# One product of an attention kernel's keys: three fp32r products of high and low parts replaced by one native fp32 product

## The reference, cut to what matters

```
q_big = einsum('bshk,hkq->bshq', q_hk, w_kc_q)
q_r   = einsum('bshq,hqr->bhsr', q_big, W_qr)
k_r   = einsum('bld,hdr->bhlr', kv_rope, W_kr)      # the keys' product
scores = einsum('bhsr,bhlr->bhsl', q_r, k_r)
attn  = softmax(scores)
ctx_c = einsum('bhsl,bld->bhsd', attn, kv_rope)
```

## Time and profile before

| | |
|---|---|
| median of 3 runs | 674.84 us (673.44 to 675.44) |
| the profiled execution's own time | 677.15 us |
| its span, first to last instruction | 675.4 us |
| mean granted TensorE clock | 0.995 |
| PE busy | 653.5 us (97%), 2870 instructions |
| DVE busy | 543.9 us (81%) |
| ACT busy | 356.8 us (53%) |
| POOL busy | 259.7 us (38%) |

### The profile page before, as it was taken

The page is one execution under the profiler, slowest core; times in us unless marked ns, Lnnn a source line. Parts: engine busy times, 40 slices in busy tenths (PEclk is TensorE's granted clock), DMA queues, the critical chain, the costliest instruction groups (busy, mean ns, idle before and its releaser), DMA issues.

```text
span 675.4 us, 9297 instructions
## 1 busy us (share of the span) xinstructions
PE 653.5 (97%) x2870; PEld 377.5 (56%) x2870; DVE 543.9 (81%) x882; ACT 356.8 (53%) x571; POOL 259.7 (38%) x232
## 2 busy tenths in 40 slices
PE   9798999999999999999999999999999898999997
PEld 8564555665665555565655555555555454445553
DVE  5787877788868885888698979997999886998873
ACT  3564664455445544554545454545454533498875
POOL 4822265133223222322235443332333352686651
PEclk9999999999999999999999999999999998999999
DMA  8108885788498849884988688869688763000001
GB/s 299 63 1 218 234 226 117 226 237 228 108 241 243 220 105 243 231 215 109 239 245 207 184 225 237 212 168 238 163 214 230 172 149 101 1 0 32 17 33 48
DMA packets 45206, 112.77 MB, mean 167 GB/s; under 512 B 11888, under 2 KB 15088, under 8 KB 45040
## 3 DMA queue, kind: packets, MB, share of 16 engines
q1 hardware_dynamic: 43712, 110.01, 61.5%
q10 hardware_dynamic: 1392, 2.29, 1.0%
q0 software_dynamic: 64, 0.00, 0.0%
HBM read 45.16 MB, written 2.10 MB: 70 GB/s over the span
## 4 chain that ended last, share of the span: by engine, by line
PE 48%; DVE 30%; ACT 7%; SPq 6%; POOL 3%; issue 3%; DMA 2%; PEld 1%; POOLq 0%; DVEq 0%; ACTq 0%; PEldq 0%
DVE E L1765 9%; PE ps_b L1392 9%; PE ps_s L1371 7%; DVE small L1755 7%; PE ps_ctx L1392 7%; ACT E L1580 6%; SPq L1096 5%; PE ps_s L586 5%; DVE wq L1781 2%; PE ps_b L1265 2%; POOL E L1160 2%; DVE x_sb L1745 2%; PE ps_b L1267 2%; PE ps_b L637 2%; PE ps_b L1266 2%
## 5 line engine op out<-in xcount | busy, mean ns | idle before, releaser
L1160 POOL TENSOR_SCALAR E<-E,small 128x1024 f32<-128x1024 f32 x128 | 151.1, 1190 | 346.7 <-DVE small L1760 346.6
L1580 ACT ACTIVATE E<-ps_s,small 128x1024 f32<-128x1024 f32 x128 | 142.3, 1113 | 209.0 <-DVE small L1755 177.5
L1765 DVE STREAM_TRANSPOSE E<-E 128x1024 f32<-128x1024 f32 x124 | 152.8, 1233 | 27.9 <-POOL E L1160 27.8
L1755 DVE TENSOR_REDUCE small<-ps_s 128x1 f32<-128x1024 f32 x128 | 149.1, 1203 | 4.5 <-PE ps_s L1371 4.4
L1392 PE MATMUL ps_ctx<-G,kv 128*128 128x512 f32 x256 | 123.2, 599 | 0.0
L1392 PE MATMUL ps_b<-G,kv 128*128 128x512 f32 x256 | 119.9, 598 | 2.1 <-DMA G<-E 2.1
L1392 PEld LDWEIGHTS ps_b<-G,kv 128*128 128x128 f32 x256 | 48.0, 190 | 51.8 <-issue 46.0
L1392 PEld LDWEIGHTS ps_ctx<-G,kv 128*128 128x128 f32 x256 | 46.4, 189 | 43.0 <-issue 40.3
L1265 PE MATMUL ps_b<-b_hi,ctx_hi 128*128 128x512 f32 x128 | 66.4, 519 | 0.6 <-DVE ctx_lo L1717 0.6
L1371 PE MATMUL ps_s<-k_hi,q_hi 64*128 64x512 f32 x256 | 57.3, 443 | 4.6 <-ACT E L1580 3.6
L586 PE MATMUL ps_s<-wq,q12T 128*128 128x512 fp8e4 x256 | 61.1, 385 | 0.1
(11 more groups left out here) (199 smaller groups left out, 960.9 us busy)
## 6 DMA issues: line engine op xcount, KB each, us to landing
G<-E SPq DMA_DIRECT2D x496, 128.0 KB, 2.4
w_stage<-in_wffn SPq DMA_DIRECT2D x48, 512.0 KB, 4.4
wo_s<-in_woT SPq DMA_DIRECT2D x8, 512.0 KB, 5.3
wq_s<-in_wq SPq DMA_DIRECT2D x7, 512.0 KB, 6.3
wkcq_s<-in_wkcqT SPq DMA_DIRECT2D x7, 384.0 KB, 4.5
out<-x_sb SPq DMA_DIRECT2D x8, 256.0 KB, 2.0
x_sb<-in_x SPq DMA_DIRECT2D x3, 512.0 KB, 5.9
wqr_s<-in_wqr SPq DMA_DIRECT2D x7, 192.0 KB, 5.4
```

Source lines behind the costliest of these rows:

```text
L1160: nc.gpsimd.tensor_scalar(e, e, rowinv[:, k:k + 1], 1.0, ALU.mult, ALU.mult).then_inc(scaled, 1)
L1580: nc.scalar.activation(out, scores, ACT.Exp, bias=negmax[:, k:k + 1], accum_out=rowsum[:, k:k + 1]).then_inc(exp_done, 1)
L1755: nc.vector.tensor_reduce(negmax[:, k:k + 1], ps_s[:, t % 2, :], AX_X, ALU.max, negate=True).then_inc(max_done, 1)
L1765: nc.vector.transpose(e_tile(w % 2, t), e_tile(w % 2, t)).then_inc(blocks_turned, 1)
```

## The change

The keys' task becomes one native fp32 product of `wkr_s` and a single transposed context `kvT`. The splits of the weights (one ACT and one DVE instruction per pair) and of the transposed context (four DVE instructions in the prologue) go; ACT's copy of the transposed context now writes the fp32 tile. PE waits for the load of the weights itself. The reload of `wkr_s` waits for the last `k` task of the pair and stands in unit 2 of SP's program in place of unit 1; the first reload waits until the prologue's `k` tasks are done.

```diff
@@ sp_pair
                     load_wq(sp, p + 2)
-                    sp.wait_ge(wk_ready, p + 2)
+                if w == 2 and not (variant == "last" or isinstance(p, int) and p == 6):
+                    sp.wait_ge(side_done, side_index(p, variant, ("k", 1, 1)) + 1)
                     load_kr(sp, p + 2)
@@ block.sync
             load_wq(sp, 1)
-            sp.wait_ge(wk_ready, 1)
+            sp.wait_ge(side_done, 8)
             load_kr(sp, 1)
@@ side_matmuls
             elif kind == "k":
                 _, b, j = task
-                pe.wait_ge(wk_ready, 1 if at is not None else p + 2)
+                pe.wait_ge(ld_kr, 16 if at is not None else 16 * p + 32)
                 ...
-                wh = wk_hi[:, :, :].rearrange("p a r -> p (a r)")
-                wl = wk_lo[:, :, :].rearrange("p a r -> p (a r)")
-                nc.tensor.matmul(into, wh, kvT_hi[:, b, cols], start=True, stop=False)
-                nc.tensor.matmul(into, wl, kvT_hi[:, b, cols], start=False, stop=False)
-                last = nc.tensor.matmul(into, wh, kvT_lo[:, b, cols], start=False, stop=True)
+                last = nc.tensor.matmul(into, wkr_s[:, :, :].rearrange("p a r -> p (a r)"), kvT[:, b, cols], start=True, stop=True)
@@ act_pair
-                    if (w, c) == WK_AT and variant != "last":
-                        wk_high(act, 16 * p + 32)
@@ block.scalar
-            def kvt_high(g):
+            def kvt_copy(g):
                 b, half = divmod(g, 2)
                 act.wait_ge(kvt_psum, g + 1)
-                copy_act(key_columns(kvT_hi[:, b, half * NF:(half + 1) * NF]), by_tile(KVT_BANK[g])).then_inc(kvthi_ready, 1)
+                copy_act(key_columns(kvT[:, b, half * NF:(half + 1) * NF]), by_tile(KVT_BANK[g])).then_inc(kvt_ready, 1)
                 ...
-            wk_high(act, 16)
@@ dve_pair
-                    if (w, c) == WK_AT and variant != "last":
-                        wk_low(dve, p + 2)
@@ block.vector
             stats(0)
-            wk_low(dve, 1)
-            kvt_low(0)
             dve.wait_ge(pow_done, 1)
             normed_row(0)
             normed_row(1)
-            kvt_low(1)
             ...
             inv_tile(dve, 0, 0, 1)
-            kvt_low(2)
             max_tile(dve, 0, 0, 2)
             max_tile(dve, 0, 0, 3)
             inv_tile(dve, 0, 0, 2)
-            kvt_low(3)
             inv_tile(dve, 0, 0, 3)
```

More of the change, by code:

```diff
@@ L99 @@
 TASK_FIRST = (SECOND_HALF_STEP, FIRST_HALF_STEP)
-WK_AT = (0, 1)
 MEAN_TASK = ("a",)
@@ L242, in build @@
         xnT = sa("xnT", [P, 2, DT, SEQ], F32R)
-        kvT_hi = sa("kvT_hi", [P, BATCH, LCTX], F32R)
-        kvT_lo = sa("kvT_lo", [P, BATCH, LCTX], F32R)
+        kvT = sa("kvT", [P, BATCH, LCTX])
         k_hi = sa("k_hi", [P, BATCH, LCTX], F32R)
@@ L259, in build @@
         mz = sa("mz", [P, 2, P])
-        wk_hi = sa("wk_hi", [P, 2, R], F32R)
-        wk_lo = sa("wk_lo", [P, 2, R], F32R)
         wkr_s = sa("wkr_s", [P, 2, R])
@@ L332, in build @@
         ln_var, ln_bias, rope_pool = (sem(n) for n in ("ln_var", "ln_bias", "rope_pool"))
-        kvt_psum, kvthi_ready, kvt_ready = (sem(n) for n in ("kvt_psum", "kvthi_ready", "kvt_ready"))
+        kvt_psum, kvt_ready = sem("kvt_psum"), sem("kvt_ready")
         xn_high, xn_split, xn_joined = (sem(n) for n in ("xn_high", "xn_split", "xn_joined"))
@@ L337, in build @@
         side_done, side_hi, side_freed = sem("side_done"), sem("side_hi"), sem("side_freed")
-        wkhi_ready, wk_ready = sem("wkhi_ready"), sem("wk_ready")
         scores_done, max_done, exp_done, inv_done, scaled = (
@@ L1563, in xn_high_part @@
             copy_act(hi, full).then_inc(xn_high, 1)
-        def wk_high(act, ready):
-            act.wait_ge(ld_kr, ready)
-            copy_act(wk_hi[:, :, :], wkr_s[:, :, :]).then_inc(wkhi_ready, 1)
         def exp_tile(act, p, w, t):
@@ L1668, in _ @@
             copy_act(mz[:, 1, R:P], prologue_bank(0)[:, P:P + R]).then_inc(pro_m, 1)
-            kvt_high(0)
-            kvt_high(1)
+            kvt_copy(0)
+            kvt_copy(1)
             act.wait_ge(side_done, 2)
@@ L1681, in _ @@
             task(5)
-            kvt_high(2)
-            kvt_high(3)
+            kvt_copy(2)
+            kvt_copy(3)
             exp_tile(act, 0, 0, 2)
@@ L1746, in side_low @@
             last.then_inc(side_freed, 1)
-        def wk_low(dve, ready):
-            dve.wait_ge(wkhi_ready, ready)
-            lo_part(wk_lo[:, :, :], wkr_s[:, :, :], wk_hi[:, :, :]).then_inc(wk_ready, 1)
         def max_tile(dve, p, w, t):
@@ L1866, in task @@
                 side_low(dve, 0, "first", PROLOGUE_TASKS[i], prologue_bank(i), at=i, hi_at=i - 2)
[L1868 to L1872, removed]
             def first_copy(c):
```

## The result

The changed kernel takes **677.59 us** (median of 11 runs, 675.64 to 679.73). The kernel before, run alternately with it, takes 674.68 us (11 runs, 672.84 to 675.44). The ratio is 1.0045, with a 95% interval from 1.0028 to 1.0061: slower, by 2.9 us. The forecast was 677.1 us, +2.25.

A forecast was written before the change was run, and what follows sets the result against it. PE was taken to bound from 68.1 to 334.4 us and DVE from there to 541. Terms +2.25 (PE) + 0 (DVE) + 0 (prologue) gave +2.25 on the median 674.84: 677.1 us, range 675.0 to 679.6.

The forecast's parts named there:

- The task's price: Each k task on PE: one native product of 0.855 us replaces three of 0.695 together, 0.16 us dearer.
- Rival 3: Native product's x2 is double listing, so it costs 0.43 us and a task gains 0.27: 670.3 us; chance 0.03.
- four passes in number: Native product on PE makes four passes, each cheaper than an fp32r product: 0.855 us, not 4 x 0.232 = 0.93.
- Bound by PE: 68.1 to 334.4 us, pairs 0 to 3: PE bounds, 14 k tasks count in full, +2.25 us.
- Pair 3's first: First k task of pair 3, hidden by the exchange's landing: 0; with a quicker landing it counts too, +0.16 us.
- Bound by DVE: 334.4 to 541 us: wk_lo's removal -0.54, PE's lag in pairs 5 and 6 +0.54; together 0, from -0.5 to +1.0.
- Rival 1: PE bounds all the way, all 28 tasks in the pairs count: +4.5, 679.3 us; chance 0.14.
- Rival 4: Pairs bound by DVE give time back: wk_lo's 0.54 gained, PE's lag absorbed; +1.7, 676.6 us; chance 0.11.
- Prologue: Before pair 0: slower first products against kvT_lo's removal, -0.27 us by the scores at 32.30, then spent; sum 0, -1.1 to +0.4.
- the microsecond that would have spoken against the forecast: Sign at pair 0's q: a start a microsecond away from 68.1 us would show the forecast wrong.
- Rival 2: Prologue: busier PE avoids the 3.41 us half-clock stretch, -1.1 us; total +1.15, 676.0 us; chance 0.16.
- Moved loads: Reload of wkr_s later in SP's queue: waits are met, 0; a stall would cost at most +4 us.

The follow-up runs named there:

- e2: Kernel before with the native product in the k tasks of pairs 0 to 3 only, nothing removed: 678.08 us, 1.0049.
- e1: The kernel before, unedited, run again to list clock and span of each execution: 673.82 us, 0.9992.
- e9: Kernel before plus eight unread identity products on PE in pair 0, ahead of unit 1's first value product: 673.90 us, 0.9983.
- e10: As e9, plus five such products in pair 7 ahead of the first product that uses the last exchange: 673.94 us, 0.9980.
- e3: Kernel before with the native product in the k tasks of pairs 4 to 6 only, low parts still made: 675.29 us, 1.0012.
- e11: Changed kernel plus the early one-column ACT activation and eight unread identity products on PE in pair 0: 675.42 us, 1.0011.
- e5: Changed kernel plus a one-column ACT activation before ACT's wait for the first side task: 676.85 us, 1.0031.
- e7: Kernel before with only the reloads of the keys' weights moved as in the changed kernel: 674.12 us, 0.9992.
- e8: Kernel before, three products kept, one kvT_lo split put behind two maxima and wk_lo made on POOL instead of DVE: 675.62 us, 1.0009.
- e6: Kernel before with two fp32r products per k task, the third (wk_hi kvT_lo) left out, losing some precision: 673.31 us, 0.9979.

## Why the prediction was right

**The task's price, +0.16.** Right. Against the profile before, which has no wait of PE there either, the changed kernel's score groups in pair 2 go from +0.84 to 1.02 over the task at (0, 3), to 1.18 over that at (1, 1), and to 1.50 over the two last. Rival 3, one record, is dead: 0.86 by starts. The prediction's "by this trace four passes in number" was no reading of the trace, though: it shows two records per product, and passes not at all.

**Bound by PE, 14 tasks, +2.25.** Right in kind; 15 tasks count. Pair 3's first, which I held to be hidden by the landing, counted in the profile after, since no wait stood before its q. The step named that condition. The forecast's 2.25 would be 2.4 without pair 3's late landing. e2 gives 2.4 + 0.4. In pair 1 the windows were to grow by 0.64 as in pair 2; they grew by 1.2, since a wait stands ahead of pair 1's q that neither the profile before nor e1 has:

```profile
135.85 0.50 PE L1336 MATMUL ps_b<-xnT,a_hi 128*128 128x512 f32 x1 [0.31 <-DVE b_lo L1702]
```

This exchange landed 3.32 us behind its last issue, and it makes 0.58 us between the score groups 7a and 7b, counted as in the table. e9 and e10, whose k tasks are the old ones, have a wait at the same q too, and e2 one at pair 4's: it comes from the exchange, not from the price of a task.

**Bound by DVE, 0.** Right, and by its parts. The changed kernel is 1.69 late against e1 before the q of pair 4 and 1.67 late at the last scores. Relief shows behind the exchanges of pairs 5 and 6 as -0.40 and -0.75; taking off the 0.11 and 0.15 by which a first task had just made it late, -0.29 and -0.60, in place of -0.54 for both. PE's lag then adds 0.49 in pair 5 and 0.31 in pair 6, in place of 0.54 for both. So -0.89 and +0.80: each side was larger than forecast by half, and that the sum is still near 0 is luck as much as insight. DVE's waits from 334.4 to 541 us hold a line that neither the profile before nor e1's has:

```profile
DVE small L1736 <- PE ps_s L1363: 0.7, 3, 0.3
```

Rival 1 (all 28 count) is dead by e3, which kept 0.53 of its twelve tasks' 1.9, and by this stretch. Rival 4 falls with the same numbers: relief and lag were both real and cancelled.

**Prologue, 0.** The sum may have held; the profiles don't resolve it, and one part was missed. First scores: +0.65 against the profile before, where 2 x 0.16 = 0.32 was forecast. The other 0.33 is the table load in this execution, which moved onto the chain because the edit removed the activation that had carried it; e2 and e11 are as late there by landings alone. I had looked at wk_hi only for who waits for its result. The Trainium skill (ScalarE: Activation LUTs, What ACT_TABLE_LOAD costs) gives 1283 ns for the load and 1380 for a drain with it; the trace agrees on the load, 1.28 us, and shows no drain here, since the copy starts at 12.06, 0.02 behind its end. kvT_lo's removal then gives most of it back: +0.06 at the third group, where I had -0.27. e11 shows the same gain, but e5, where x landed late, does not. The scores that were to start near 32.0 start at 32.36, and pair 0's q at 67.30 for 68.1, near the microsecond that would have spoken against the forecast; most of that is the missing half-clock stretch.

**Rival 2, the prologue's clock.** Its step is in the profile after: no stretch at 33.4, and the fourth score group goes from +0.06 to -0.85, a gain of 0.91 for the 1.1 worked out. But e1 and e7 lack that stretch too, with the old products. It comes and goes from one execution to the next; a rival built on one profile's clock had chance for cause. The Trainium skill (TensorE: Matmul & The Clock Gate, Part 1) has activity release the throttled state. e9's clock fits that: with PE's gap before pair 0's q filled, it stayed up in 12 of 12 executions; that extra products keep it up in the prologue, as the rival needs, no run tested.

**Moved loads, 0.** Right (e7).

**The sum.** 2.4 (pairs 0 to 3) + 0 (pairs 4 to 6) + 0.1 (prologue with the table load; at unit 2 it is +0.32 against e1 and -0.05 against e7) is the 2.5 of the equal clocks. The agreement is closer than the evidence: left out are pair 1's wait, 0.58 that e7 doesn't have, and the last exchange. Against e7, a profile of the old products without a half-clock stretch, the changed kernel is 2.9 us late at the last scores and 2.0 at the end, for e7 waits 2.69 us for that exchange and the changed kernel 1.28. So the forecast is right in its main term, which e2 shows by itself; that it came within 0.5 us of the median is in part chance.

What stays open: why an exchange lands 2.3 us after its last issue in one pair and execution and 4.0 in another; it moves pair 3's q by 1.4 us, the first product behind the last exchange by about as much, and is as large as half the effect. The relation of e8's slower exchange to its earlier start was seen once, not varied. And the change costs 2.5 us at equal clock without the filled wait, 1.25 with it.

## What to carry to other kernels

Price a matrix product by the distance of starts and by its records, in its own data type: here three reduced products cost less than one exact one. The same 0.16 us counted in full where PE never waits, by about a quarter where DVE and PE hand over (0.53 of e3's 1.9), and not at all before a wait, so place comes before price; and a saving in the same place is worth only what the next engine leaves (e6). Before removing an instruction ask what rides on it: here the first activation carried the table load. Compare executions at equal granted clock, and more than one profile of the same kernel, before explaining a microsecond. If the clock falls behind a short wait of PE, products that nobody reads are worth a try: they made the clock steady in one kernel here and helped the other little.

## What the runs showed of the hardware

- Behind a wait of PE of 2.2 us the granted clock was 0.51, the 1.2 GHz level, for the next 3.4 us (e1), and behind one of 3.1 us it was 0.50 for 6.8 us (e8). Not always: the changed kernel waited 2.08 us at e1's place, and e7 2.69 us ahead of the last exchange, and both kept 1.00. With sixteen short records, 1.8 us, in the first of these waits, the kernel before was at full clock in 24 of 24 executions, the changed kernel in 8 of 12.
- A native fp32 product of 128 x 128 by 128 x 512 is 0.86 us in two records wherever I read it, in both kernels; an fp32r product of that shape is 0.23 us in one.
- The load of ACT's table came with the first activation of the program, but not always ahead of its wait: before, it ran at 4.44 us while wk_hi waited for its weights until 9.36; after, it stood behind the wait for the m task, at 10.76. With an activation of one column ahead of that wait it ran at 4.23 again (e5). Why the two orders differ was not tried.
- The same exchange of 16 DMAs landed 2.3 or 4.0 us behind its last issue, in two pairs of one execution.
